# Expert layer 1 of a metaformer block on Trainium2: fp16 hi/lo token products replaced by f32 quadrant matmuls, and GELUs over 1024 columns

## What is computed

```python
top_p, top_idx = jax.lax.top_k(softmax(xt @ Wr + br), 2)
weights = top_p / top_p.sum(axis=-1, keepdims=True)
xn = (xt - mu) * jax.lax.rsqrt(var + LN_EPS)
xe = xn[None, :, :] * ln_g[:, None, :] + ln_b[:, None, :]
h = gelu(einsum('end,edh->enh', xe, W1) + b1[:, None, :])      # D=64 -> H=256, E=8
y = einsum('enh,ehd->end', h, W2) + b2[:, None, :]
out = (weights[:, :, None] * sel).sum(axis=1)                   # sel: the two chosen experts
```

## Time and profile before

| | |
|---|---|
| median of 3 runs | 228.63 us (228.62 to 231.39) |
| span of the profiled execution | 227.4 us; what lies around it is taken as 1.2 us, the median less the span |
| TensorE busy | 206.7 us (91%) |
| ScalarE, VectorE, GpSimd busy | 128.1, 123.8, 47.0 us |
| mean granted TensorE clock | 0.981 of 2.4 GHz |

### The profile page before, as it was taken

How to read it: one execution, slowest core, us unless ns; L and a number is a source line. 1 busy time by engine, 2 the same in 40 slices (tenths; PEclk the granted TensorE clock), 3 DMA queues, 4 the chain that set the end, 5 groups by cost and what they waited for, 6 DMA issues and landing times.

```text
span 227.4 us, 4913 instructions
## 1 busy us (share of the span) xinstructions
PE 206.7 (91%) x2096; PEld 113.6 (50%) x2096; DVE 123.8 (54%) x232; ACT 128.1 (56%) x207; POOL 47.0 (21%) x50
## 2 busy tenths in 40 slices
PE   7699788999976898988899799999999999999993
PEld 3395667566334577963524244444444444444430
DVE  0582055659949977999731633554334553334555
ACT  2256942035338553669685387666786666786640
POOL 5560393040069992030400000000000000000000
PEclk9979999999999999999699999999999999999998
DMA  6990000000000000000005953260804508063001
GB/s 219 294 265 14 0 3 6 3 0 7 0 0 4 0 3 0 3 0 0 3 0 164 220 128 69 82 151 0 184 3 108 122 4 184 0 150 84 0 0 46
DMA packets 6596, 14.35 MB, mean 63 GB/s; under 512 B 2736, under 2 KB 4144, under 8 KB 5680
## 3 DMA queue, kind: packets, MB, share of 16 engines
q1 hardware_dynamic: 6576, 14.06, 24.7%
HBM read 12.87 MB, written 1.18 MB: 62 GB/s over the span
## 4 chain that ended last, share of the span: by engine, by line
PE 68%; ACT 9%; DMA 7%; POOL 6%; DVE 6%; SPq 1%; issue 1%; POOLq 1%; DVEq 0%
PE psum L710 22%; PE psum L694 21%; PE psum L538 7%; DMA xs<-in_x 3%; DMA wide<-gate_store 2%; PE psum L512 2%; POOL place L920 2%; ACT place L747 2%; PE psum L634 2%; PE psum L548 2%; PE psum L424 2%; POOL place L926 2%; ACT hid L861 1%; POOL place L919 1%; PE psum L557 1%
## 5 line engine op out<-in xcount | busy, mean ns | idle before, releaser
L694 PE MATMUL psum<-tok,w1s 128*64 128x512 f16 x512 | 60.8, 383 | 1.3 <-ACT hid L861 0.8
L1160 DVE SCALAR_TENSOR_TENSOR term<-psum,sm,wide 128x512 f32<-128x512 f32 x32 | 24.0, 750 | 62.1 <-PE psum L710 51.6
L861 ACT ACTIVATE hid<-psum,b1p 128x512 f32<-128x512 f32 x64 | 38.2, 701 | 16.7 <-PE psum L694 16.3
L694 PEld LDWEIGHTS psum<-tok,w1s 128*64 128x64 f16 x512 | 28.7, 110 | 35.9 <-issue 9.1
L861 ACT ACTIVATE w1f<-psum,b1p 128x512 f32<-128x512 f32 x32 | 19.6, 688 | 17.1 <-PE psum L694 17.0
L710 PE MATMUL psum<-hid,w 128*64 128x512 f32 x128 | 28.9, 593 | 0.0
L1165 DVE TENSOR_TENSOR x<-x,term 128x512 f32<-128x512 f32 x32 | 22.1, 692 | 1.1
L861 ACT ACTIVATE w1g<-psum,b1p 128x512 f32<-128x512 f32 x32 | 19.7, 714 | 0.2
L710 PEld LDWEIGHTS psum<-hid,w 128*64 128x64 f32 x128 | 9.1, 137 | 15.1 <-issue 9.4
L710 PE MATMUL psum<-w1g,w 128*64 128x512 f32 x64 | 15.1, 594 | 1.4 <-DVE term L1160 1.4
L538 PE MATMUL psum<-h_pad,tap_bd 64*64 64x512 f32 x144 | 15.9, 589 | 0.0
(11 more groups left out here) (147 smaller groups left out, 295.4 us busy)
## 6 DMA issues: line engine op xcount, KB each, us to landing
wide<-gate_store SPq DMA_DIRECT2D x14, 512.0 KB, 6.4
xs<-in_x SPq DMA_DIRECT2D x2, 512.0 KB, 5.6
w1f<-in_W SPq DMA_DIRECT2D x2, 512.0 KB, 10.0
block_out<-x SPq DMA_DIRECT2D x4, 256.0 KB, 6.4
wide<-gate_store SPq DMA_DIRECT2D x2, 384.0 KB, 5.1
c<-const SPq DMA_DIRECT2D x1, 548.5 KB, 4.4
hid<-in_W1T SPq DMA_DIRECT2D x1, 512.0 KB, 10.3
w<-in_W SPq DMA_DIRECT2D x1, 512.0 KB, 11.8
```

The source lines that it names most:

```text
L694: mm = pe.matmul(h_bank(n)[side * H:(side + 1) * H, :], w1s[:, part, e, k * P + side * H:k * P + (side + 1) * H], tok[:, pair, half, b, :] ...
L861: act.activation(hid_of[u % 4][:, t, :], h_bank(n), ACT.Gelu, bias=b1p[:, e * KT + k:e * KT + k + 1]).then_inc(gelu_ready, 1)
L1160: dve.scalar_tensor_tensor(term[:, u % 2, :], y_bank(u), b2t[:, e:e + 1], gate_b[part][:, e % (E // 2), :], ALU.add, ALU.mult).then_inc(te ...
```

## The change

Tokens stay f32. `features` transposes `xc` itself, `keep_tokens` copies f32; `high_part`, `low_part`, the fp16 weights and the fp16 constant go. `up(u)` has two tiles per unit, one per hidden half, each a whole slot of two banks (image b in bank b): 4 matmuls of 64 rows and 64 output columns, in the order rows 0-63 to columns 0-63, 64-127 to 64-127, 0-63 to 64-127, 64-127 to 0-63. One GELU reads the 1024 columns of both banks. The first-layer tiles have one slot for units 0 to 3 and three slots after; both y banks are in `slot(0, 0)`. `hid` has three sets, the fourth is `w1f`.

```diff
-        h_early = [bank(slot(0, 1), 0), bank(slot(0, 1), 1)]
-        h_late = h_early + [bank(slot(1, 1), 0), bank(slot(1, 1), 1), bank(slot(1, 0), 1), bank(slot(0, 0), 0)]
-        y_banks = [bank(slot(0, 0), 1), bank(slot(1, 0), 0)]
+        h_early = [slot(0, 1)]
+        h_late = h_early + [slot(1, 1), slot(1, 0)]
+        y_banks = [bank(slot(0, 0), 1), bank(slot(0, 0), 0)]
...
             def features(p):
-                pe.wait_ge(const16_in, 16)
                 pe.wait_ge(logits_read, p + 1)
-                to = slot(p, 1).bitcast(F16)
                 for j in range(TT):
                     if j % 4 == 0:
-                        pe.wait_ge(parts_ready, 2 * p + j // 4 + 1)
-                    for b in range(B2):
-                        a = (j // 4 * 2 + b) * CHUNK + j % 4 * P
-                        mm = pe.transpose(to[:, a:a + P], parts[p][:, (j * 2 + b) * P:(j * 2 + b + 1) * P], ident16)
+                        pe.wait_ge(xn_ready, 2 * p + j // 4 + 1)
+                    mm = pe.transpose(slot(p, 1)[:, j * P:(j + 1) * P], xc[p][:, j * P:(j + 1) * P], ident)
...
-                for t in range(TILES):
-                    k, b = divmod(t, B2)
-                    n = TILES * u + t
-                    before = last_in(h_bank, n)
+                moving = bank(tok[:, pair, :], half)
+                for k in range(KT):
+                    n = KT * u + k
+                    before = last_in(h_slot, n)
                     if before >= 0:
                         pe.wait_ge(gelu_ready, before + 1)
-                    for part in range(2):
-                        for side in range(2):
-                            mm = pe.matmul(h_bank(n)[side * H:(side + 1) * H, :],
-                                           w1s[:, part, e, k * P + side * H:k * P + (side + 1) * H], tok[:, pair, half, b, :],
-                                           start=part == 0, stop=part == 1)
+                    for swapped in range(2):
+                        for b in range(B2):
+                            side = crossed(b, swapped)
+                            mm = pe.matmul(bank(h_slot(n), b)[rows_of(side), :],
+                                           w1g[rows_of(b), e, k * P + side * H:k * P + (side + 1) * H], moving[rows_of(b), :],
+                                           start=True, stop=True)
                     mm.then_inc(w1_done, 1)
...
-            def high_part(p):
-                for j in range(2):
-                    act.wait_ge(xn_ready, 2 * p + j + 1)
-                    act.copy(part_of(p, 0, j), split(bank(xc[p], j), H)).then_inc(high_ready, 1)
...
-                for t in range(TILES):
-                    k = t // B2
-                    n = TILES * u + t
+                for k in range(KT):
+                    n = KT * u + k
                     act.wait_ge(w1_done, n + 1)
-                    act.activation(hid_of[u % 4][:, t, :], h_bank(n), ACT.Gelu,
+                    act.activation(hid_of[u % 4][:, B2 * k:B2 * (k + 1), :].rearrange("p b n -> p (b n)"), h_slot(n), ACT.Gelu,
                                    bias=b1p[:, e * KT + k:e * KT + k + 1]).then_inc(gelu_ready, 1)
...
-            def low_part(p):
-                for j in range(2):
-                    pool.wait_ge(high_ready, 2 * p + j + 1)
-                    pool.tensor_tensor(part_of(p, 1, j), split(bank(xc[p], j), H), part_of(p, 0, j), ALU.subtract).then_inc(parts_ready, 1)
...
-                link(pool.tensor_tensor(w1g[:, :, :], w1f[:, :, :], lng.unsqueeze(2).broadcast_to([P, E, HID]), ALU.mult))
-                link(pool.tensor_copy(w1s[:, 0, :, :], w1g[:, :, :]))
-                pool.tensor_tensor(w1s[:, 1, :, :], w1g[:, :, :], w1s[:, 0, :, :], ALU.subtract).then_inc(w1_ready, 1)
+                pool.tensor_tensor(w1g[:, :, :], w1f[:, :, :], lng.unsqueeze(2).broadcast_to([P, E, HID]), ALU.mult).then_inc(w1_ready, 1)
```

More of the change, by code:

```diff
@@ L53 @@
     "inverse_over_kh": (35, 40), "keep_back": (24, 27), "keep_half": (25, 28), "square_tokens": (26, 31),
-    "mix_branches": (16, 18), "inverse_over_kw": (36, 41), "high_part": (29, 92), "tokens": (37, 43),
-    "residual": (19, 22), "norm_tokens": (21, 24), "keep_tokens": (30, 93), "features": (42, 92), "low_part": (6, 7),
+    "mix_branches": (16, 18), "inverse_over_kw": (36, 41), "tokens": (37, 43),
+    "residual": (19, 22), "norm_tokens": (21, 24), "keep_tokens": (30, 93), "features": (42, 92),
     "router": (39, 91), "route": (23, 25), "gates_to_rows": (101, 102), "shares": (26, 27), "biases": (20, 20),
@@ L119, in constants @@
     out[:, CONST["small_index"]] = np.arange(E, 0, -1)[None, :]
-    return out, np.eye(P, dtype=np.float16)
+    return out
 SMALL = {}
@@ L156, in small_weights, with metaformer @@
     return out
-def metaformer(nc, x, small, W1, W1T, ln_b, W2, const32, const16, out):
+def metaformer(nc, x, small, W1, W1T, ln_b, W2, const32, out):
     ctx = ExitStack()
@@ L198, in metaformer @@
         c32 = sb("c32", [P, CONST_N])
-        c16 = sb("c16", [P, P], F16)
         def const(name):
@@ L224, in metaformer @@
         w1g = sb("w1g", [P, E, HID])
-        w1s = sb("w1s", [P, 2, E, HID], F16)
         w2 = sb("w2", [P, NT, H])
@@ L233, in metaformer @@
         x1 = sb("x1", [P, PAIRS, N])
-        tok = sb("tok", [P, PAIRS, 2, B2, TT // 2 * P], F16)
+        tok = sb("tok", [P, PAIRS, N])
         still = sb("still", [P, CHUNK], F16)
@@ L255, in metaformer @@
         back = x_conv
-        parts = [x_conv[p].bitcast(F16) for p in range(PAIRS)]
         h2 = [place[4][:, p, :] for p in range(PAIRS)]
@@ L267, in metaformer, with h_slot @@
         mix = [wide[1][:, p, 0:N].rearrange("p (g n) -> p g n", n=H) for p in range(PAIRS)]
-        h_early = [bank(slot(0, 1), 0), bank(slot(0, 1), 1)]
-        h_late = h_early + [bank(slot(1, 1), 0), bank(slot(1, 1), 1), bank(slot(1, 0), 1), bank(slot(0, 0), 0)]
-        y_banks = [bank(slot(0, 0), 1), bank(slot(1, 0), 0)]
+        h_early = [slot(0, 1)]
+        h_late = h_early + [slot(1, 1), slot(1, 0)]
+        y_banks = [bank(slot(0, 0), 1), bank(slot(0, 0), 0)]
         TILES = B2 * KT
         EARLY = 2 * AHEAD
-        def h_bank(n):
-            early = EARLY * TILES
+        def h_slot(n):
+            early = EARLY * KT
             return h_early[n % len(h_early)] if n < early else h_late[n % len(h_late)]
@@ L288, in last_in @@
             return max((k for k in range(n) if which(k) is which(n)), default=-1)
-        hid = sb("hid", [P, 2, TILES, CHUNK])
-        hid_of = [hid[:, 0], hid[:, 1]] + [w[:, :, :].rearrange("p (t a) n -> p t (a n)", t=TILES) for w in (w1f, w1g)]
+        hid = sb("hid", [P, 3, TILES, CHUNK])
+        hid_of = [hid[:, 0], hid[:, 1], hid[:, 2], w1f[:, :, :].rearrange("p (t a) n -> p t (a n)", t=TILES)]
         gate_b = [wide[n][:, 0, :].rearrange("p (e n) -> p e n", n=CHUNK) for n in range(2)]
@@ L297, in metaformer @@
         gate_store = nc.dram_tensor("gate_store", (PAIRS, 2, B2, E * CHUNK), F32)
-        def part_of(p, part, j):
-            return parts[p].rearrange("p (t a h) -> p t a h", a=2, h=H)[:, j * K:(j + 1) * K, part, :]
         def shifted(p, b, tap):
@@ L309, in metaformer @@
         dct_in = sem("dct_in")
-        const_in, const16_in, weights_in = sem("const_in"), sem("const16_in"), sem("weights_in")
+        const_in, weights_in = sem("const_in"), sem("weights_in")
         ffn_in, out_done = sem("ffn_in"), sem("out_done")
@@ L330, in metaformer @@
          attn_ready, y_ready, yt_ready, mix_ready, xout_ready, back_ready, half_ready, x1_ready, csq_ready, xn_ready,
-         high_ready, parts_ready, wr_centred_ready, logits_read, tok_ready, gap_ready, tanh_ready, gparts_ready, gates_ready, coef_ready) = (sem(n) for n in (
+         wr_centred_ready, logits_read, tok_ready, gap_ready, tanh_ready, gparts_ready, gates_ready, coef_ready) = (sem(n) for n in (
              "sq_ready dh_ready dw_ready xd_ready h1_ready halo_ready xt_ready gram_ready prod_ready tk_ready "
@@ L334, in metaformer @@
              "attn_ready y_ready yt_ready mix_ready xout_ready back_ready half_ready x1_ready csq_ready xn_ready "
-             "high_ready parts_ready wr_centred_ready logits_read tok_ready gap_ready tanh_ready gparts_ready gates_ready coef_ready").split())
+             "wr_centred_ready logits_read tok_ready gap_ready tanh_ready gparts_ready gates_ready coef_ready").split())
         w1_done, gelu_ready, w2_done, term_done, add_done, gates_out = (
@@ L707, in down @@
                 for k in range(KT):
-                    pe.wait_ge(gelu_ready, TILES * u + B2 * (k + 1))
+                    pe.wait_ge(gelu_ready, KT * u + k + 1)
                     for b in range(B2):
@@ L832, in keep_tokens @@
                     act.wait_ge(tok_done, 2 * p + j + 1)
-                    act.copy(tok[:, p, j, :, :].rearrange("p b n -> p (b n)"),
-                             slot(p, 1).bitcast(F16)[:, j * N:(j + 1) * N]).then_inc(tok_ready, 1)
```

(11 more changed lines are left out.)

4 lines of the change are left out of this document (1 added, 3 removed).

## The result

The changed kernel takes 242.13 us (median of 4 runs, 238.63 to 242.87) against 228.62 before: ratio 1.048, 95% interval 1.037 to 1.059, slower. The forecast was 237.3 with a range to 242.0, so the direction was right; the median lies 0.1 us above the range's end, and three of the four executions lie above it. The profiled execution took 242.22 us with a span of 240.2, 12.8 more than the span of before (it is one of the longer ones; the shortest, 238.63, had a span of 236.6 and a mean clock of 0.971).

The account below looks back on a forecast made before the run. TensorE was taken to bound the kernel (68% of the chain). Tiling changes 4.7, later gates' copy 3.4 and clock 0.6 made 8.7 us on a 227.4 span, 236.1, plus 1.2 around it: 237.3 us, range 232.0 to 242.0.

Parts of the forecast that it names:

- Matmul time of `up`: `up` in each round: four f32 quadrant matmuls cost the same as before, 3.44 us for two units against 3.45.
- Changes of tiling: Rounds, between `up` and `down`: 26 tiling changes drain TensorE, 0.36 us per round over 13 rounds, 4.7 us more.
- Start, pair 0: Start of the experts: without roundings and subtractions `up(0)` starts 1.5 us earlier, first GELU at 101.3, 1.0 us gained.
- One slot: Units 0 to 3: each tile waits for the previous GELU, 2.34 us per tile; gates' copy 3.4 us later.
- From the copy to `down(3)`: DMAs and waits after the gates' copy: one chain that moves with it, `down(3)` at 132.0 for 128.60.
- Clock: TensorE in the starved first units: one or two tiles at the lower clock, 0.6 us more, bounds 0 and 6.9.
- rival B: First units: the lower clock holds through both starved stretches, 6.9 us, giving 243.6 us; chance 0.12.
- Rival C: First units: TensorE refills while GELU reads, GELUs run back to back; not slower, 225.6 us with free tiling changes; chance 0.05.
- Rival A: Rounds: changes of tiling are free in this order, rounds stay 6.87 us, giving 232.6 us; chance 0.18.

Follow-up runs that it names:

- the repeat: The changed kernel once more with no edit, on the chip of the experiments: 240.06 us, ratio 1.045.
- a_hold: Changed kernel with three idle fp16 matmuls ahead of each TensorE wait for the one slot in units 0 to 3, two behind router(1): 235.55 us.
- b_hold: Kernel before the change with three idle fp16 matmuls behind router(1): 228.48 us, ratio 0.996.
- b_gates: Kernel before the change with the gates' transposes and their copy moved between units 2 and 3: 227.02 us, ratio 0.988.
- the pair of alternating versions: Down, up, down, up in each round from the third on, in the changed kernel (244.16 us) and the kernel before (229.51 against 229.42).
- a_bankwise: Changed kernel with units 0 to 3 waiting, filling and running their GELU bank by bank, 512 columns each: 235.07 us, ratio 1.021.

## Why the prediction was right, and where it was short

- **Matmul time of `up`**: right. A round is 7.50 with four changes and 7.17 with two, so 6.84 with none, where the kernel before has 6.88.
- **Changes of tiling**: right in place and kind, a little dear. 0.36 per round from the earlier trace rows, measured 0.29; the 26 changes cost 3.79 us, not 4.7. The row with 64*64 to 128*64 (0.16) was the better one; the 0.20 of 128*128 to 64*64 did not carry over. The Trainium skill (TensorEngine Tiling, section Key Properties) says that a change of tiling mode drains TensorE. The traces agree with it in both directions, at 0.15 us a change; they show the cost and that no weights are loaded ahead, not the draining itself.
- **Start, pair 0**: right, and to 0.1 us by luck. First GELU at 101.44, predicted 101.3; but it came at 99.81 in the repeat and at 101.77 in a_hold, and at 101.0 instead of 102.33 in the kernel before in b_hold and b_gates.
- **One slot**: right. 2.33 per tile, predicted 2.34; GELU 1.11, predicted 1.13. With the clock held the copy is at 121.81, predicted 121.8, but with a first GELU 0.47 later than predicted: from that GELU to the copy it is 20.04, predicted 20.5. The difference is VectorE's routing: from its first step to the tanh it takes 3.13 us (112.80 to 115.93) where it was 3.84, 0.7 less and not 0.3. Net of the earlier start (0.89), one slot cost 3.1 us and not 3.4.
- **From the copy to `down(3)`**: 10.5 us after the gates' store for 9.9 before, of which 0.5 is a gate load that took 6.22 for 5.68. a_hold had 5.64 there and the repeat of the same kernel 5.62, so this is how loads differ and not the change.
- **Clock**: this is the step that failed. "One or two tiles at the lower clock ... 0.6 us" measured 5.3 us in the profiled execution and 6.2 in the repeat's. The prediction counted tiles only. The router (1.6 us more), the token transposes (0.9) and four tiles at 0.85 each lie in one line on TensorE with the waits between, and only little of it is hidden by the tanh, which itself waits for the router. Its bound of 6.9 and rival B (243.6) covered it. By the prediction's own sign, more than 5 us at 0.5 in 101 to 122 us, it is B that came (10.2 us in one stretch), and the 242.13 lies nearer to B's 243.6 than to 237.3; what B said of the first tiles of unit 0 did not come, they kept the full clock. The first three tiles (two in the repeat) kept it while TensorE worked 0.86 of each 2.33 us; that it would not last was to be weighed more, since the change lowers TensorE's work exactly where before it had already lost the clock for 3.4 us.
- Sum: 3.8 changes of tiling, 3.1 one slot net of the earlier start, 5.3 clock, 0.5 loads are 12.7; the spans differ by 12.8. The prediction's 8.7 lacks 4.7 of the clock and 0.5 of loads, and had 0.9 too much for the changes and 0.3 for the slot. That the time still comes to the edge of the range owes something to luck: the two terms that were too dear hide 1.2 us of the miss. It also took 1.2 us for what lies around the span. The profiled execution's own time is not on record; the runs of the kernel before beside the experiments, which list both time and span, have 2.1 to 2.5, and the profiled execution of the changed kernel has 2.0. This is in the absolute time and not in the difference of the spans.
- Rival C is excluded by its own sign: the copy is at 126.79 and not ahead of 118.4, and the GELUs are 2.33 us apart, with each tile waiting for the whole GELU before it. Rival A is excluded by rounds of 7.17 and by the pair of alternating versions.

What is open: why the lower level begins where it does. Executions of one kernel differ in it, and no run here isolates what makes it begin. Open too is what the 0.15 us of a change is made of.

## What to carry to other kernels

Where TensorE is the chain, count its time from start to start over a whole round, forms of tiling included: two stages that fill the array equally well cost more by turns when one splits the rows and the other does not, here 0.15 us at each seam. A wide instruction on another engine that takes a whole double-bank buffer removes the overlap where there is only one such buffer, and it saves nothing where that engine was idle anyway. And where a change makes TensorE wait, price every stage that follows in its stream at the lower clock, not the waiting tiles alone.

## What the runs showed of the hardware

- A change between 64*64 and 128*64 tilings costs 0.15 to 0.16 us in both directions, and a change of operand type in one tiling nothing (1.71 to 1.73 for 1.72). Across a change the first weight load is not ahead of its matmul; without one it was 0.43 us ahead.
- An ACTIVATE over 1024 f32 columns of two PSUM banks takes 1.11 us alone, 0.15 less than two of 512 back to back (1.26, a_bankwise).
- Three idle fp16 matmuls per wait (a_hold, 0.82 us in their record) kept the granted clock at 1.0 over 107 to 128 us, where it was 0.51 to 0.52 for 17 us, and made the kernel 4.5 to 6.6 us faster though TensorE did more. The same trick behind the router of the kernel before left the clock falling in its profile and gained nothing by the clock: its executions took 228.6 us at mean clocks of 0.991 and of 1.000 alike.
- While GpSimd subtracted, VectorE's steps beside it in the kernel before took up to 0.81 us where they took 0.29 in the changed one (L1103 at 110.15, L1076 at 113.77).
